# Splitting the first query stacks of two attentions, the first attention's stacks and the seam inside the second mixture

## The chip, the cores and the metric

The kernel runs on one core of a Trainium2 chip. The metric is the device time of one execution in microseconds (us), the median of three runs. The core has five engines that run side by side: TensorE (PE in the profile, with its weight loads as PEld), VectorE (DVE), ScalarE (ACT), GpSimd (POOL) and SyncE (SP, which only issues transfers). They meet through semaphores that the kernel sets and waits for by hand. Instructions of one engine run in the order in which they were written.

## The reference

Four pairs of an attention and a mixture of experts, each added to a residual stream `x` of B x S = 4 x 256 tokens, 128 wide, after a layer norm without weights:

```python
x = x + _L0_xattn_ref(_layernorm(x), ctx_1024, ...)   # 8 heads of 16, lengths mask keys and queries
x = x + _L0_ffn_ref(_layernorm(x), ...)               # shared expert + top 2 of 8, tanh gelu
x = x + _L1_xattn_ref(_layernorm(x), ctx_1024, ...)   # 8 heads of 128, relative positions
x = x + _L1_ffn_ref(_layernorm(x), ...)               # inner norm, mix, norm, then top 2 of 8, silu
x = x + _L2_xattn_ref(_layernorm(x), ctx_1024, ...)   # 16 heads of 8, a 256 x 256 mask
x = x + _L2_ffn_ref(_layernorm(x), ...)               # top 2 of 8, relu
x = x + _L3_xattn_ref(_layernorm(x), ctx_1024, ...)   # 16 heads of 8, biases
x = x + _L3_ffn_ref(_layernorm(x), ...)               # top 1 of 8, gelu
```

An attention is softmax(Q K^T) V and an output projection, with keys and values from `ctx_1024`. An expert is a 128 -> 512 -> 128 network; the mixture adds the results of the best one or two experts of each token, weighted. All is fp32.

## The kernel before, in words

The parts are called `a0, f0, a1, f1, a2, f2, a3, f3` (ORDER, L308): attentions `a`, mixtures `f`. Tokens stand in 8 tiles of 128; a half is 4 tiles (512 tokens), and a sequence (256 tokens) is 2 tiles. Each engine has a function of its own (sync L329, gpsimd L556, vector L708, scalar L1283, tensor L1542), and each walks the parts in ORDER. Within a part all engines run the same loop over steps `i` or `s`, and what is done in which step is written out by hand. A step number therefore fixes what stands before and behind an operation in its engine's queue.

*Narrow attentions* (`a0`, `a2`, `a3`; L816, L1331, L1609). Scores are wanted in fp32 exactness from bf16 matmuls: queries and keys are each split into three bf16 parts (`split`, L784: four VectorE steps), the parts are written to a scratch in HBM (`stack_out`, L354, three DMAs) and read back so that the parts of one head stand below each other in the partitions of `Qs` and `Ks` (`stack_in`, L372). One unit `i` of the loop is one head of one sequence: `scores` on TensorE (L1636), a maximum on VectorE (L878 or L875), GpSimd splits the maxima of four units (`maxima_parts`, L645), TensorE turns them (`turn_maxima`, L1651, from unit 6), ScalarE copies them and, in `a2` and `a3`, SP sends them into rows of `Qs` (L402). Then come the shifted scores (L1669, LAG units later), exponentials (L1363), probabilities times values (L1688), a transpose, normalising, an output transpose, the projection (L1716) and the residual (L856). In `a0` the queries come by halves and the keys at once; in `a2` and `a3` the first half of the queries is made in the mixture before, and the second half within the attention, at unit SECOND_HALF = 13, since the second half of `x` is only then combined (`combine`, L892).

*Mixtures* (`mixture`, L1073, L1423, L1819). Each half goes through: norm (`norm_stats`, `norm_apply`, with the power by GpSimd, `layer_norm_rstd` L592), transpose (`turn_norm`), ScalarE's copy (`copy_T`), `logits` (L1573), `choose` (L915, which experts), `ranks` (L1755), `slots` (L936, each token's row in a list sorted by expert), `plan_blocks`. GpSimd scatters the rows (`send_rows` L614, one indirect DMA for each tile and rank), SP reads the sorted rows (`rows_in`, L459) in quads of four blocks of 128, TensorE turns a quad (L1825) and does one block a step: `up_block(s - 1)` (L1835) and `down_block(s - 2)` (L1864), with ScalarE's activation between them. Blocks 8 and up of a half ("more") take an expert that is chosen at run time: VectorE copies its weights one step ahead (`fetch_weights`, L1081). VectorE adds a quad's biases (`finished`, L1092), SP writes it back (`y_out`, L470), GpSimd gathers the rows of each token (`fetch_results`, L624) and VectorE adds them to `x` (`combine`, L992). There are nb = 19, 15, 15 and 11 blocks a half in `f0` to `f3`, and 2 nb + 2 steps. The first quad of half 1 is turned in step nb - 1 (`quads_at`, L111). In `f1` and `f2` the keys and values of the next attention are made from step 11 on; half 0 is combined and normed for it in step nb + 9 and nb + 10, transposed in nb + 11, made to queries in nb + 12 and split in nb + 13. `f1` has an inner layer before its routing (`inner_layer`, L1241, L1923).

*Queues.* SP's order of transfers is written out (L409 to L552): a wait there holds all transfers behind it. GpSimd's order follows `norms` (L121, L666): behind the norm of `a2.0` stand the gathers of `f1`'s second half, mixed with the first maxima (L674). At the start ScalarE fills `Va` (L1314) and 32 rows of `Qs` (L1317), and VectorE 32 rows of `Ks` (L770).

## Time and profile before

| | us |
|---|---|
| median of three runs | 806.21 |
| lowest, highest run | 806.12, 817.81 |
| profiled execution | 808.12 |
| its span | 806.4 |
| TensorE, VectorE, ScalarE, GpSimd busy | 634.6, 415.5, 373.7, 184.8 |
| chain that ended last: PE, DVE, DMA, POOL, issue, ACT | 48%, 15%, 12%, 9%, 8%, 5% |

Times in the trace count from the start of the span. A row of the timeline has its start, how long its instructions lasted, engine, line and operation, what it writes and reads, how many instructions it merges, and in brackets the engine's idle time before it with what ended it. The chain is followed back from the last instruction, at each step to what released it.

### The profile page before, as it was taken

What the parts mean: (1) busy time and instruction counts of PE and PEld (TensorE: products, weight loads), DVE (VectorE), ACT (ScalarE), POOL (GpSimd) and SP (SyncE); (2) the same over time, 40 slices, a digit from 0 to 9 for tenths busy, and PEclk for the clock granted to TensorE, in tenths of its full rate; (3) what the DMA queues carried; (4) which work ended last, traced back from release to release, by engine and by line L of the source; (5) the groups of instructions that cost most, each with busy time, mean ns of one, the idle gap of its engine ahead of it and who ended that gap; (6) DMA issues with size and microseconds to landing.
All of it is one profiled execution on the core that took longest, in us unless ns stands there. A gap on an engine that the chain in (4) does not pass through costs nothing.

```text
span 806.4 us, 14301 instructions
## 1 busy us (share of the span) xinstructions
PE 634.6 (79%) x4784; PEld 486.8 (60%) x4784; DVE 415.5 (52%) x1410; ACT 373.7 (46%) x930; POOL 184.8 (23%) x352
## 2 busy tenths in 40 slices
PE   4398659998898988687756589987997469978790
PEld 2165459886665666586755347755996324546790
DVE  6675533524266678656123567772544277873320
ACT  7065225554464546764443146653332126755460
POOL 1234313030040010413120411132313051131111
PEclk8599679999999999989797679997998759998996
DMA  5894089110677771201491313324174413431211
GB/s 155 252 358 158 13 166 189 33 37 27 163 244 217 230 213 53 76 14 50 148 144 53 75 43 73 112 90 89 54 202 79 102 31 85 154 102 43 76 50 49
DMA packets 92978, 90.76 MB, mean 113 GB/s; under 512 B 10980, under 2 KB 83301, under 8 KB 92716
## 3 DMA queue, kind: packets, MB, share of 16 engines
q1 hardware_dynamic: 89324, 82.51, 38.0%
q0 software_dynamic: 3584, 7.35, 3.6%
q8 instruction: 40, 0.66, 0.3%
q14 instruction: 30, 0.25, 0.1%
HBM read 53.06 MB, written 35.59 MB: 110 GB/s over the span
## 4 chain that ended last, share of the span: by engine, by line
PE 48%; DVE 15%; DMA 12%; POOL 9%; issue 8%; ACT 5%; SPq 1%; DVEq 0%; POOLq 0%; ACTq 0%
PE bank L1854 10%; PE bank L1875 9%; PE bank L1696 4%; PE bank L1644 3%; DMA late<-rows_sorted,idx 3%; PE bank L1679 3%; POOL rows_sorted L621 3%; PE bank L1983 2%; PE bank L1790 2%; DMA rows_sorted<-stage 2%; DVE negmax L878 2%; PE bank L1950 2%; POOL xm L631 2%; PE bank L1831 1%; POOL late L631 1%
## 5 line engine op out<-in xcount | busy, mean ns | idle before, releaser
L1875 PE MATMUL bank<-W,spare 128*128 128x128 f32 (+1 forms) x960 | 132.9, 284 | 1.4 <-ACT spare L1447 0.9
L1875 PEld LDWEIGHTS bank<-W,spare 128*128 128x128 f32 x960 | 122.8, 200 | 3.2 <-issue 2.1
L878 DVE TENSOR_REDUCE negmax<-bank 128x2 f32<-128x512 f32 x128 | 85.3, 689 | 48.7 <-PE bank L1644 32.0
L1644 PE MATMUL bank<-big 128*128 128x256 bf16 x320 | 73.3, 306 | 36.7 <-DMA big<-parts_scratch 26.0
L1363 ACT ACTIVATE late<-bank 128x512 f32<-128x512 f32 x120 | 70.8, 595 | 56.6 <-PE bank L1684 26.9
L1447 ACT ACTIVATE spare<-bank,W 128x128 f32<-128x128 f32 x224 | 64.0, 372 | 41.5 <-PE bank L1854 41.5
L621 POOL DMA_INDIRECT rows_sorted<-xn,idx x56 | 55.6, 992 | 109.2 <-DVE idx L955 94.6
L1679 PE MATMUL bank<-big 128*128 128x256 bf16 x320 | 74.6, 284 | 2.6 <-ACT late L1363 1.2
L1644 PEld LDWEIGHTS bank<-big 128*128 128x128 bf16 x320 | 28.6, 105 | 65.8 <-issue 36.7
L1495 ACT ACTIVATE big<-big,r 128x256 f32<-128x256 f32 x64 | 31.9, 500 | 45.8 <-DVE r L1189 45.7
L1696 PE MATMUL bank<-late 128*32 128x256 f32 x480 | 44.7, 399 | 0.1
L1560 PE MATMUL bank<-ident,xn 128*128 128x128 f32 x64 | 14.7, 355 | 35.0 <-DVE xn L733 21.8
L1983 PE MATMUL bank<-big,QKT 128*128 128x128 f32 x256 | 34.7, 278 | 8.8 <-DVE x_res L1204 7.4
L631 POOL DMA_INDIRECT late<-rows_sorted,idx x24 | 22.8, 952 | 73.3 <-DMA rows_sorted<-QKT 35.9
L1679 PEld LDWEIGHTS bank<-big 128*128 128x128 bf16 x320 | 29.9, 101 | 16.0 <-ACT late L1363 3.8
L1983 PEld LDWEIGHTS bank<-big,QKT 128*128 128x128 f32 x256 | 31.1, 191 | 11.0 <-issue 9.1
L1350 ACT ACTIVATE nmT<-bank 12x256 bf16<-12x256 f32 x40 | 14.5, 363 | 47.2 <-PE bank L1655 47.1
L653 POOL CAST nmp<-negmax 128x8 bf16<-128x8 f32 x40 | 7.6, 191 | 122.7 <-DVE negmax L878 70.6
L1560 PEld LDWEIGHTS bank<-ident,xn 128*128 128x128 f32 x64 | 9.6, 169 | 41.8 <-issue 26.0
L595 POOL TENSOR_SCALAR rstd<-mv 128x4 f32<-128x4 f32 x20 | 5.2, 258 | 127.7 <-DVE mv L726 127.6
L1854 PE MATMUL bank<-stage,W 128*128 128x128 f32 x256 | 33.8, 275 | 0.0
L1189 DVE CUSTOM_DVE_ANT_0 big<-bank,late 128x256 f32<-128x256 f32 x64 | 24.4, 420 | 18.2 <-PE bank L1953 13.7
(280 smaller groups left out, 1372.6 us busy)
## 6 DMA issues: line engine op xcount, KB each, us to landing
W<-in_f_wx SPq DMA_DIRECT2D x25, 578.0 KB, 7.2
late<-bands_scratch SPq DMA_DIRECT2D x8, 1024.0 KB, 5.5
W<-in_f_wx SPq DMA_DIRECT2D x8, 514.0 KB, 3.5
bands_scratch<-zrow SPq DMA_DIRECT2D x4, 768.0 KB, 12.7
big<-parts_scratch SPq DMA_DIRECT2D x6, 512.0 KB, 5.5
stage<-rows_sorted SPq DMA_DIRECT2D x11, 256.0 KB, 3.3
rows_sorted<-stage SPq DMA_DIRECT2D x11, 256.0 KB, 3.3
parts_scratch<-big SPq DMA_DIRECT2D x3, 768.0 KB
```

The source lines that it names most:

```text
L621: pool.indirect_dma_start(rows_sorted[hf], bass.IndirectOffsetOnAxis(idx[:, k, t:t + 1], 0), xn[:, t, :], None)\
L631: pool.indirect_dma_start(gathered(key, hf)[:, t, k, :], None, rows_sorted[hf], bass.IndirectOffsetOnAxis(idx[:, k, 4 * hf + t:4 * hf + t ...
L878: ins = v.tensor_reduce(negmax[:, g % 2, :, j], bank[i % 2][:, :].rearrange("p (t k) -> p t k", t=2), AX.X, ALU.max, negate=True)
L1363: a.activation(PTs[j % NPT][:, :, :], bank[2 + j % 2][:, :].rearrange("p (c q) -> p c q", c=2), ACT.Exp)\
L1447: ins = a.activation(hidB[n % 3][:, c, :], src[:, 128 * c:128 * (c + 1)], func, bias=b1r[:, c:c + 1])
L1495: a.activation(Pw[2 * (i % 2) + j], negS[2 * (i % 2) + j], ACT.Exp, bias=r1[:, k:k + 1], scale=-1.0, accum_out=r2[:, k:k + 1]).then_inc(se ...
L1644: ins = mm(o, Qs[:, h, S * b + 128 * t:S * b + 128 * (t + 1)], Ks[:, h, S * b:S * (b + 1)], start=True, stop=not mask)
L1679: ins = mm(o, Ks[:, h, S * b + 128 * c:S * b + 128 * (c + 1)], Qs[:, h, S * b:S * (b + 1)], start=True, stop=key == "a3")
L1696: ins = mm(dst[32 * j:32 * (j + 1), 0:256], Va[:, 2 * b + c, h + j, :], PTs[(4 * g + j) % NPT][:, c, :], start=c == 0, stop=c == 1)
L1854: ins = mm(dst[:, 128 * c:128 * (c + 1)], w[:, 128 * c:128 * (c + 1)], rhs, start=True, stop=True)
L1875: ins = mm(dst[:, 128 * place_:128 * (place_ + 1)], hidB[n % 3][:, c, :], w2[:, 128 * c:128 * (c + 1)], start=c == 0, stop=c == FC - 1)
L1983: ins = mm(dst[:, 128 * j:128 * (j + 1)], PTw[i % 2][:, 256 * j + 128 * c:256 * j + 128 * (c + 1)], Vp[:, 2 * b + c, 128 * (2 * p + j):128 ...
```

## The change

It does six things. (1) Start: the stacks of `a0` go by halves, keys too; the fills of the rows of `Qs` and `Ks` are both ScalarE's, as fp32 copies, and `Va` is filled behind the first queries; VectorE's fill is gone. (2) `f0`: in `a0`'s loop `copy_T`, `logits`, `choose`, `ranks` and `slots` of half 0 stand one to three steps earlier, and logits ahead of the step's attention work. In every mixture the logits of half 1 stand at the head of their step. (3) `f1`: the inner layer's end, logits and choice of half 1 two steps earlier (a clear by ScalarE moves from step 6 to 8); the first quad of half 1 is turned in step nb + 1, behind the down block of the step before; on SP `y_out("f1", 0, 3)` stands ahead of `rows_in("f1", 1)`. (4) `a2` and `a3`: the first half's queries are made in two pieces, "0" (sequence 0) and "h" (sequence 1), each with norm, transpose, queries, split and stack of its own; `combine` of half 0 goes by two tiles; gathers and maxima alternate on GpSimd. (5) SECOND_HALF is 15. (6) `f3`: `rows_in("f3", 1)` ahead of `y_out("f3", 0, 1)`. Semaphores are merged and renamed to make room. The core of the diff (left out: renamed semaphores, and helpers that put the pieces' tile and column ranges in place of `4 * hf`):

```diff
 MASK_ROW = 96
 MAX_ROW = 80
-SECOND_HALF = {"a2": 13, "a3": 13}
...
             starts = [(hf, q, max(hf * all_blocks[key] + SHARED[key] + 4 * q - 1, 0)) for hf in range(2) for q in range(quads[key])]
+            starts = [(hf, q, all_blocks[key] + 1 if (key, hf, q) == ("f1", 1, 0) else at_step) for hf, q, at_step in starts]
             return [(hf, q) for hf, q, at_step in starts if at_step == s]
 
...
         COUNTS["x"] = [("a0", B), ("a1", NT), ("a2", B), ("a3", B)]
 
@@ -278,6 +281,34 @@
                 return stage
             return {"f0": big[:, 8192:10240], "f1": late[:, 4096:6144]}.get(key, QKT)
 
+        def tiles_of(name):
+
+
+            key, hf = name.split(".")
...
-            stack_out("a0", 1)
+            stack_out("a0", 1, 0)
             stack_out("a0", 0, 0)
-            stack_in("a0", 1)
+            stack_in("a0", 1, 0)
             stack_in("a0", 0, 0)
+            stack_out("a0", 1, 1)
             sp.wait_ge(sem("c.maskrow"), 1)
             sp.dma_start(Ks[MASK_ROW:MASK_ROW + 1, 1:8, :], Ks[MASK_ROW:MASK_ROW + 1, 0:1, :].broadcast_to([1, 7, TOK]))\
               .then_inc(sem("ld.mask"), 16)
-            stack("a0", 0, 1)
-            sp.wait_ge(sem("c.zrow"), 1)
+            stack_out("a0", 0, 1)
+            stack_in("a0", 1, 1)
+            stack_in("a0", 0, 1)
+            sp.wait_ge(sem("c.zrow"), 2)
...
             rows_in("f1", 0)
             for q in range(3):
                 y_out("f1", 0, q)
+            y_out("f1", 0, 3)
             rows_in("f1", 1)
-            y_out("f1", 0, 3)
             def attention_transfers(key, before, nxt):
 
+                stack(key, 0, 0)
                 y_out(before, 1, 2)
-                stack(key, 0, 0)
+                stack_out(key, 0, "h")
                 y_out(before, 1, 3)
+                stack_in(key, 0, "h")
                 sp.wait_ge(*at(before, "bd", 2 * all_blocks[before]))
...
             attention_transfers("a3", "f2", "f3")
             rows_in("f3", 0)
             y_out("f3", 0, 0)
+            rows_in("f3", 1)
             y_out("f3", 0, 1)
-            rows_in("f3", 1)
             y_out("f3", 0, 2)
...
-                if name in ("a2.0", "a3.0"):
-                    fetch_results(BEFORE[name[:2]], 1, [0, 1])
-                    maxima_parts(name[:2], [0])
-                    fetch_results(BEFORE[name[:2]], 1, [2])
-                    maxima_parts(name[:2], [1])
-                    fetch_results(BEFORE[name[:2]], 1, [3])
-                    maxima_parts(name[:2], [2])
+                if name in ("a2.h", "a3.h"):
+                    for t in range(4):
+                        fetch_results(BEFORE[name[:2]], 1, [t])
+                        if t < 3:
+                            maxima_parts(name[:2], [t])
...
             v.memset(zrow[:, :], 0.0).then_inc(sem("c.zrow"), 1)
-            v.memset(spare[96:128, 0:256].bitcast(bf16), 1.0).then_inc(sem("c.ones"), 1)
-            link(v.memset(big[96:128, 8192:12288], 0.0))
+            v.memset(spare[96:128, 0:256].bitcast(bf16), 1.0).then_inc(sem("c.zrow"), 1)
...
@@ -821,10 +856,11 @@
                     x_ready(dve, key, 0)
                     norm_stats(key, 0, x)
                     norm_apply(key, 0, x, xn)
-                    for c in range(2):
-                        dve.wait_ge(*at(key, "kt", c + 1))
-                        split(KT, slice(512 * c, 512 * (c + 1)), "kp")
+                    dve.wait_ge(*at(key, "kt", 1))
+                    split(KT, slice(0, 512), "kp")
                     query_parts(key, 0)
+                    dve.wait_ge(*at(key, "kt", 2))
+                    split(KT, slice(512, TOK), "kp")
                     x_ready(dve, key, 1)
...
-                    if i == 2 * H + L + 18:
+                    if i == 2 * H + L + (15 if key == "a0" else 18):
                         choose(ffn_key, 0)
-                    if i == 2 * H + L + 21:
+                    if i == 2 * H + L + (18 if key == "a0" else 21):
                         slots(ffn_key, 0)
...
-                    first = 9 if key == "f1" else 3
+                    first = 7 if key == "f1" else 3
...
-                    if s == nb + (9 if key in NEXT else 8):
+                    if key in NEXT:
+                        if s == nb + 7:
+                            combine(key, 0, (0, 1))
+                            norm_stats(nxt, 0, x)
+                        if s == nb + 8:
+                            norm_apply(nxt, 0, x, xn)
+                        if s == nb + 10:
+                            combine(key, 0, (2, 3))
+                            x_ready(dve, nxt, 0)
+                            norm_stats(nxt, "h", x)
+                        if s == nb + 11:
+                            query_parts(nxt, 0)
+                            norm_apply(nxt, "h", x, xn)
+                        if s == nb + 14:
+                            query_parts(nxt, "h")
+                    elif s == nb + 8:
                         combine(key, 0)
                         if nxt:
                             x_ready(dve, nxt, 0)
                             norm_stats(nxt, 0, x)
-                    if s == nb + (10 if key in NEXT else 9) and nxt:
+                    elif s == nb + 9 and nxt:
                         norm_apply(nxt, 0, x, xn)
                     ks = KEYS_STEP.get(key, 99)
                     if ks + 1 <= s < ks + 5:
                         keys_parts(nxt, [s - ks - 1])
                     if s == ks + 5:
                         values(nxt)
-                    if s == nb + 13 and nxt in NARROW:
-                        query_parts(nxt, 0)
...
+            ones = spare[96:128, 0:256]
+            act.wait_ge(sem("c.zrow"), 2)
+            a.activation(big[96:128, 0:4096].rearrange("p (k c) -> p k c", c=2 * D),
+                         ones.unsqueeze(1).broadcast_to([32, 16, 2 * D]), ACT.Copy).then_inc(sem("c.rows"), 1)
+            a.activation(big[96:128, 8192:12288].rearrange("p (k c) -> p k c", c=2 * D),
+                         zrow[96:128, :].unsqueeze(1).broadcast_to([32, 16, 2 * D]), ACT.Copy).then_inc(sem("c.rows"), 1)
...
+                    a.activation(Va[:, :, :, :].rearrange("p t h w -> p (t h w)").rearrange("p (k c) -> p k c", c=2 * D),
+                                 zrow[:, :].unsqueeze(1).broadcast_to([128, 16, 2 * D]), ACT.Copy).then_inc(sem("c.Va"), 1)
...
-                        if s == 6:
+                        if s == 8:
                             act.wait_ge(sem("a1.pv"), UNITS)
                             clear(Vp[:, 6:8, :].rearrange("p t (k c) -> p (t k) c", c=2 * D))
-                        if s == 8:
+                        if s == 6:
                             copy_T("f1n", 1, nT[1])
...
-                    if s == nb + 11 and nxt in NARROW:
-                        copy_T(nxt, 0, nT[0])
-                    if s == nb + 12 and nxt in NARROW:
-                        queries(nxt, 0)
+                    if key in NEXT and s in (nb + 9, nb + 12):
+                        copy_T(nxt, 0 if s == nb + 9 else "h", nT[0])
+                    if key in NEXT and s in (nb + 10, nb + 13):
+                        queries(nxt, 0 if s == nb + 10 else "h")
...
                         pe.wait_ge(sem(f"st.q{b // 2}"), 16 + 32 * LAYER_OF[key])
+                    if h == 0 and b == 1 and key != "a0":
+                        pe.wait_ge(sem("st.qh"), 32 * LAYER_OF[key])
+                    if h == 0 and b == 2 and key == "a0":
+                        pe.wait_ge(sem("st.k1"), 16)
...
+                    if key == "a0" and i == 2 * H + L + 15:
+                        logits(ffn_key, 0)
...
                 for s in range(N + 2):
+                    seam = key == "f1" and s == nb + 1
+                    if seam:
+                        down_block(s - 2)
+                    if s == first:
+                        logits(key, 1)
                     for hf, q in quads_at(key, s):
                         turned(hf, q)
...
-                    if s >= 2:
+                    if s >= 2 and not seam:
                         down_block(s - 2)
                     if key == "f1":
-                        if s in (2, 3, 8):
-                            inner_layer(1, (2, 3, 8).index(s))
+                        if s in (2, 3, 6):
...
-                    first = 9 if key == "f1" else 3
-                    if s == first:
-                        logits(key, 1)
...
-                    if s == nb + 11 and nxt in NARROW:
-                        turn_norm(nxt, 0)
-                    if s == nb + 12 and nxt in NARROW:
-                        queries(nxt, 0)
+                    if key in NEXT and s in (nb + 9, nb + 12):
+                        turn_norm(nxt, 0 if s == nb + 9 else "h")
+                    if key in NEXT and s in (nb + 10, nb + 13):
+                        queries(nxt, 0 if s == nb + 10 else "h")
```

## Rows read from the trace of the kernel before

**Rows 1.** Busy time, clock (PEclk) and transfers by stretch; (x) is a number of instructions.

```profile
0.00:37.00 37.00, 13.31 (x33) 7.21 (x34) 23.07 (x63) 15.60 (x10) 7.90 (x22) 0.72 0.75 209
...
414.00:451.00 37.00, 14.09 (x86) 12.06 (x85) 9.91 (x34) 8.27 (x25) 1.53 (x2) 0.71 0.41 82
```

**Rows 2.** Timeline of the start, all engines, 0 to 37 us.

```profile
2.08 3.62 ACT L1314 ACTIVATE late<-zrow 128x4096 f32<-128x4096 f32 x1
...
5.72 7.03 ACT L1317 ACTIVATE big<-spare 32x8192 bf16<-32x8192 bf16 x1
...
6.19 3.74 PE L1594 MATMUL bank<-cT,aw 128*128 128x512 f32 x4 [6.19 <-DMA cT<-in_ctxT]
...
12.77 1.09 ACT L1328 ACTIVATE QKT<-bank 128x512 f32<-128x512 f32 x2
...
15.05 0.69 DVE L782 TENSOR_TENSOR big<-QKT,big 128x512 bf16<-128x512 f32 x1
...
20.33 3.37 SPq L369 DMA_DIRECT2D parts_scratch<-spare  x3
...
36.92 1.01 PE L1644 MATMUL bank<-big 128*128 128x256 bf16 x4 [4.93 <-DMA big<-parts_scratch]
```

**Rows 3.** Timeline, end of the first attention, TensorE and GpSimd.

```profile
85.64 1.03 PE L1581 MATMUL bank<-rw,nT 128*128 128x8 f32 x8 [0.60 <-DVE x_res L859]
...
89.34 0.21 PE L1762 MATMUL bank<-oneh,aw 128*128 128x32 bf16 x1 [2.40 <-DVE oneh L934]
...
93.22 1.25 POOL L621 DMA_INDIRECT rows_sorted<-xn,idx  x1 [16.07 <-DVE idx L955]
```

**Rows 4.** Timeline, the seam inside the second mixture: TensorE, SyncE, GpSimd.

```profile
387.23 1.12 PE L1831 MATMUL bank<-ident,stage 128*128 128x128 f32 x4 [7.47 <-DMA stage<-rows_sorted]
...
388.14 1.92 PE L1854 MATMUL bank<-late,w1copy 128*128 128x128 f32 x8
...
393.59 1.06 PE L1854 MATMUL bank<-stage,W 128*128 128x128 f32 x8
...
396.40 0.36 SPq L474 DMA_DIRECT2D rows_sorted<-late  x1
...
399.34 0.99 POOL L631 DMA_INDIRECT late<-rows_sorted,idx  x1 [16.01 <-DMA rows_sorted<-late]
```

**Rows 5.** Timeline, seam from second mixture to third attention: VectorE, TensorE, SyncE.

```profile
411.84 0.35 DVE L1005 SCALAR_TENSOR_TENSOR x_res<-late,wts,x_res 128x128 f32<-128x128 f32 x1
...
418.08 0.35 DVE L1005 SCALAR_TENSOR_TENSOR x_res<-late,wts,x_res 128x128 f32<-128x128 f32 x1 [5.88 <-DMA late<-rows_sorted,idx]
...
427.23 1.15 PE L1560 MATMUL bank<-ident,xn 128*128 128x128 f32 x4 [12.62 <-DVE xn L733]
...
450.63 0.37 PE L1644 MATMUL bank<-big 128*128 128x256 bf16 x1 [10.07 <-DMA big<-parts_scratch]
...
442.85 1.31 SPq L382 DMA_DIRECT2D big<-parts_scratch  x2
```

**Rows 6.** Timeline, seam from third mixture to fourth attention: GpSimd, VectorE, TensorE.

```profile
600.94 0.98 POOL L631 DMA_INDIRECT late<-rows_sorted,idx  x1 [18.50 <-DMA rows_sorted<-QKT]
...
614.36 2.32 DVE L1005 SCALAR_TENSOR_TENSOR x_res<-late,wts,x_res 128x128 f32<-128x128 f32 x7 [1.92 <-DMA late<-rows_sorted,idx]
...
620.24 1.16 PE L1560 MATMUL bank<-ident,xn 128*128 128x128 f32 x4 [5.68 <-DVE xn L733]
...
642.88 1.01 PE L1644 MATMUL bank<-big 128*128 128x256 bf16 x4 [11.04 <-DMA big<-parts_scratch]
```

**Rows 7.** Transfers issued from 395 to 452 us: count, KB each, median us to landing.

```profile
big<-parts_scratch SPq DMA_DIRECT2D x1, 1024.0 KB, 13.7
...
rows_sorted<-stage SPq DMA_DIRECT2D x1, 192.0 KB, 6.4
...
late<-rows_sorted,idx POOLq DMA_INDIRECT x8, 14.0
...
xm<-rows_sorted,idx POOLq DMA_INDIRECT x1, 2.6
```

**Rows 8.** Timeline of TensorE, the seam inside the last mixture.

```profile
760.66 1.09 PE L1831 MATMUL bank<-ident,stage 128*128 128x128 f32 x4 [4.26 <-DMA stage<-rows_sorted]
```

157 lines of the change are left out of this document (90 added, 67 removed).

## The prediction

> **What bounds the kernel now.** I first read the table by stage, for TensorE's clock and idle time. TensorE is busy for 634.6 of 806.4 us, but not evenly [rows 1]. In the first 37 us it works 13.3 us, at a mean clock of 0.72; in 414 to 451, the seam from the second mixture to the third attention, 14.1 of 37 us at 0.71. So the time to be had lies where chains of small steps and transfers leave TensorE empty. Then I read what each first matmul after an empty stretch had waited for. Start: ScalarE fills two constant regions before its first key copy (ends 5.7 and 12.75), the copy starts at 12.77 although the keys' matmuls end at 9.93, and the first score is at 36.92, behind a DMA [rows 2]. Routing of the first mixture: logits start at 85.64, after the probabilities, projection and residual of the attention; slots are known at 92.3 and the first row is sent at 93.22 [rows 3]. Second mixture: TensorE waits 7.47 us for the second half's rows at 387.23 [rows 4]. First seam: 12.62 us for `xn` at 427.23 and 10.07 us for the query stack at 450.63 [rows 5]. Second seam: 5.68 and 11.04 us [rows 6]. Last mixture: 4.26 us at 760.66 [rows 8]. The six waits from 387 us on add up to 51.1 us; none is arithmetic. (The third attention is `a2`, the fourth `a3`.)
>
> **The change, part by part.** Times below are on the old trace's scale; each part's gain is carried along.
>
> *Start.* ScalarE does the 32-row fills as 4096 fp32 columns each. One 4096-column fill took 3.62 us, one of 8192 bf16 columns 7.03 [rows 2], so the two now end at 2.08 + 2 x 3.62 = 9.3 in place of 12.75; the third (`Va`) moves behind the first queries. The key copy then starts at 9.3, waits a moment for its matmul, and the first half's parts are split at 12.3 (a split of 512 columns took 2.3 us: it began behind the copy's first half, at 13.4, and its last step ended at 15.74 [rows 2]). The query chain (transpose, copy, matmul 2.07, copy 0.60, split 2.3) gives query parts at 16.7, where they were ready at 20.33 [rows 2]. Before, 4.5 MB went out and in between 18.0 and 36.9, with the DMA engines full. Now 3.0 MB must pass before the first score, and 0.75 MB of second-half keys slips in: 18.5 x 3.75/4.5 = 15.4 us from 12.8, so 28.2, and the mask row, issued at about 26 behind VectorE's second norm, lands near 30. First score: 30.7, a gain of 6.2 (bounds 3 and 8). What is late next is the second half's stack: parts at 33.4, two reads after the writes, landing near 44 to 46 (a read of 0.75 MB took 7.8 us from its first issue in the first seam [rows 5]), needed 14 us after the first score, at 45. I take 1 us off: 5.
>
> *First mixture's routing.* Logits go ahead of the transposes, probabilities and projection; the choice (VectorE, 2.6 us, from the logits' end at 86.67 to the ranks at 89.34 [rows 3]) then runs under them. The copy of the transposes could be done at 80.2, so logits end at 81.2, which delays the attention's work by 1.3 us. Ranks then wait for the residual of that group at about 86.1, not for the choice at 89.3 [rows 3]. Gain: 89.34 - 86.25 = 3.1. The second half's norm follows (it waited for the slots' bank until 92.4), and GpSimd's eight sends and one `rstd` shift with it. I take 3 (bounds 0, if the attention's end decides, and 5).
>
> *Second mixture.* Inner norm, logits and choice come two steps earlier. Two blocks are 3.6 us, but logits wait for their copy, and VectorE's weight copy of that step waits for the hidden block behind them: I get the slots at 370.1 for 372.4, rows sent at 380.1 + 2.3 = 382.4. At the seam three down and two up blocks (5 x 0.9 = 4.5 us) now run before the wait. Against this, on SP the last result write of half 0 goes ahead of `rows_in` of half 1, so rows wait for the last down block (384.9), three additions and 0.4 us of issue: received at 388.8, later than 387.23 [rows 4]. But at that moment only one transpose group stands before block 15, which comes at 390.6 in place of 393.6, though at the lower of the clock's two levels, 1.2 GHz: the same eight matmuls took 1.92 us at 388.14, behind the wait, and 1.06 at 393.59 [rows 4]. Old block 15 ran fast, the new one slow; with that counted, block 16 ends at 393.7 for 396.3. Shift: 2.6 us. The result write starts at 386 and not 396.40, so GpSimd's gathers start at 388.5 and not 399.34.
>
> *First seam.* The key stack's transfers, too, are issued 8.5 us earlier. The gathers took 14.0 us to land there and 2.6 us in the next attention [rows 7]. The first tile was consumed at 411.84, the second at 418.08 [rows 5]. If all moves by 8.5 us, tile 1 lands at 409.6; as its gathers now go out ahead of the key stack's read, it may land up to 6 us sooner. So 403.5 to 409.6, and only tiles 0 and 1 are needed at step 22. Adding, half the norm and `rstd` (3.5 us): transpose at 409.3 to 413, where TensorE is ready at 408.0, and not 427.23. Remaining: 13 blocks' halves at 0.9 = 11.7, small pieces 1.3, lower clock 0 to 2: the mixture ends at 422.5 to 428 (before 440.56). The first sequence's query parts are ready at 416 to 421, since the queries come five steps before the end; out 3.4 us, in 5 (from the first issue at 442.85 it was 7.8 us for twice the columns [rows 5]): 424.5 to 430. First score at 427.5 in the middle, before 450.63: gain 23, the 2.6 included (bounds 15 and 27).
>
> *What is given back in the third attention.* GpSimd now fetches a tile before the first maxima, and first waits for the last result write, which stands behind the first read and the "h" write on SP. It landed just as scores began, now some 3.5 us after. Tile 0 (2.5 us) and its maxima parts (1.1 us) are then done at 7.1, for a turn due at 6.7 us after the first score; the four tiles, each 2.5, with three maxima parts, end near 20 with landing, and `combine` at unit 15 comes at 16 to 17. VectorE waits about 3 us there, and a score needs its maximum. Cost 3 (bounds 0 and 8).
>
> *Second seam.* Gathers are not moved here (600.94, tile 1 consumed at 614.36 [rows 6]). With two tiles the transpose goes at 617.9, 2.3 earlier, but four more block halves (3.6 us) lie behind it: the mixture ends at 633.4, 1.6 later than before. The query stack is ready at 634.5, in place of 642.88: gain 8.4 (bounds 4 and 10). Given back in the fourth attention, where VectorE's reductions, one a unit, set the pace and nothing hides a wait: 3.5 (bounds 0 and 8).
>
> *Logits at the head of their step in mixtures 1, 3, 4.* TensorE waits 0.85 us for the copy, and no longer 0.78 for the choice: nothing. In the last mixture, slots come 1.3 us earlier and `rows_in` no longer stands behind a result write: rows at 757.7 for 760.66, and less idle time before them. Gain 3 (bounds 1 and 4). Renamed semaphores and the two moved clears: nothing, since ScalarE still does each within the wait for the next block; without that cover a clear costs its own length once.
>
> *A rule weighed against the trace.* In the seam the gathers were slow only while SP's queue was full [rows 7]. The Trainium skill (DMA: Bandwidth & Descriptors, "Queues, rings and completion order") says that each DMA engine takes the queues that have work in turn, packet by packet; the trace's 14.0 against 2.6 us agrees. By that rule the order on either queue counts for little and the whole knot moves, so tile 1 would land 8.5 us earlier, at the late end of the interval above, which lengthens the sum's gap before the transpose by 3 us. The same page ("Rules for kernel authors") asks for transfers of 1 MiB or more; the change halves them, and no row before shows a piece of 256 columns. If pieces were no faster than halves, each stack would cost 1.5 us more, 3 in all.
>
> **Sum.** 5 + 3 + 23 - 3 + 8.4 - 3.5 + 3 = 35.9. The profiled execution took 808.12, 1.7 more than its span of 806.4; the sum gives it 772.2. The median of the runs was 806.21, so the forecast is 806.2 - 35.9 = 770 us, rounded.
>
> **The rivals.** (A) *Transfers keep their length.* The knot at the first seam moves whole (first score at 432, 18.5 gained), both given-back terms are 6, and the start waits 3 for the second stack: 3 + 3 + 18.5 - 6 + 7 - 6 + 2 = 21.5, 785 us. For it: the pieces keep their number of rows, and the gathers' 14.0 us shows full queues. Against: the key stack's read landed after 13.7 us and half as many bytes after 7.8 [rows 5, 7]. (B) *The earlier order frees more.* Gathers land before the key stack is read at all, no transpose waits, and TensorE keeps its clock through both short gaps: 7 + 4 + 27 - 1 + 10 - 1 + 4 = 50 less 3 for late second halves, 759 us. Against: after each wait of over 4 us shown the first matmuls ran at 1.2 GHz (1.92 us for eight [rows 4]). (C) *Slower: maxima behind results.* In both attentions `maxima_parts` of group 0 stands on GpSimd behind the last result write, itself behind two stack transfers on SP. If it lands L us after the first score, the stall is L + 3.6 - 6.7. The gains outside are 42.4; it decides from 21.2 a seam, L = 24. The worst landing of a read here, 13.7 us [rows 7], taken twice (read and result) with a write of 3 between, begun 2 us before the first score, gives L = 28: stalls of 25 each, 806.2 - 42.4 + 50 = 814 us. Against: in the old seam the same write landed after 6.4 us, behind a whole read [rows 7]. (D) *The change does less than it says:* the choice is early, but in the seams another wait (weights copied by VectorE while it stands at `combine`) takes all but 12 us: 794.
>
> **Chances.** Forecast 0.53 (own range 764 to 777), A 0.22, B 0.16, C 0.04, D 0.05. The range 757 to 787 takes in A and most of B. Two per cent, about what a measurement can tell from no change, is 16 us: faster 0.91, within 0.06 (D and some of C), slower 0.03.
>
> **What would show it.** First score near 31; `choose` of mixture 1 under the probabilities; in mixture 2 block 15 right behind the wait; the gathers starting 10 us before block 23; TensorE idle under 5 us before the `a2.0` transpose and under 4 before each first score; VectorE waiting for a gather at unit 15 in both attentions. A first score above 435 on the old scale, or stalls over 8 us in an attention, would prove the forecast wrong.

## The result, and the profile after

The changed kernel took 778.42 us (median of four runs, 772.52 to 783.57) beside 806.16 for the kernel before: a ratio of 0.9674, with a 95% interval of 0.9571 to 0.9777. By the medians it is 28 us faster, by the ratio 26. A later session of three rounds gave 777.76 beside 807.42 us, a ratio of 0.9652 (0.9614 to 0.9689): 30 and 28 us. The forecast was 770 with a range of 757 to 787: right in sign and inside the range, with 36 us forecast and 26 to 30 measured. Ratios, here and below, leave out the executions marked slow (one of `rows_first`, 789.91 us, and one of the kernel before, 2087 us, in each of the last two sessions), while medians keep them.

The first profiled execution took 783.57 us (span 781.8), the one of the later session 774.13 (span 772.4). Both are used below, since they differ by 9 us for the same program. Line numbers are those of the changed kernel, and in the experiments those of each run's own kernel.

The start, timeline (ScalarE, VectorE, TensorE), answers to [rows 2]:

```profile
5.60 3.60 ACT L1369 ACTIVATE big<-zrow 32x4096 f32<-32x4096 f32 x1
9.22 1.09 ACT L1380 ACTIVATE QKT<-bank 128x512 f32<-128x512 f32 x2
...
29.26 1.06 PE L1706 MATMUL bank<-big 128*128 128x256 bf16 x4
34.00 3.27 PE L1706 MATMUL bank<-big 128*128 128x256 bf16 x10 [3.68 <-DVE negmax L914]
...
31.78 0.69 DVE L817 TENSOR_TENSOR spare<-QKT,spare 128x512 bf16<-128x512 f32 x1
...
33.27 0.67 DVE L914 TENSOR_REDUCE negmax<-bank 128x2 f32<-128x512 f32 x1
```

The first score is at 29.26, 7.7 us earlier. But two units on, TensorE stands for 3.68 us: VectorE is still at the second half's query parts and the masks, and its first maximum starts at 33.27. What is carried on is 3.7 us: the first matmul with the values is at 43.89, before at 47.57.

Routing of the first mixture, timeline, TensorE and GpSimd, answers to [rows 3]. Logits no longer wait for the residual, the ranks (82.70) do:

```profile
82.70 0.18 PE L1826 MATMUL bank<-oneh,aw 128*128 128x32 bf16 x1 [0.61 <-DVE x_res L895]
...
102.87 1.11 PE L1896 MATMUL bank<-ident,big 128*128 128x128 f32 x4 [5.42 <-DMA big<-rows_sorted]
...
86.41 1.25 POOL L657 DMA_INDIRECT rows_sorted<-xn,idx  x1 [12.95 <-DVE idx L991]
```

The seam inside the second mixture and the first seam, timeline, TensorE, SyncE, GpSimd and VectorE, answers to [rows 4, 5]:

```profile
383.45 1.15 PE L1940 MATMUL bank<-W,spare 128*128 x8 [0.44 <-ACT spare L1502]
388.99 0.99 PE L1896 MATMUL bank<-ident,stage 128*128 128x128 f32 x4 [4.38 <-DMA stage<-rows_sorted]
...
410.43 0.49 PE L1614 MATMUL bank<-ident,xn 128*128 128x128 f32 x2 [0.91 <-DVE xn L768]
...
426.13 0.27 PE L1706 MATMUL bank<-big 128*128 128x256 bf16 x1
...
433.40 0.29 PE L1717 MATMUL bank<-identb,nmp 128*12 128x128 bf16 x2 [2.22 <-POOL nmp L692]
...
447.52 0.39 PE L1706 MATMUL bank<-big 128*128 128x256 bf16 x1 [2.81 <-DVE negmax L914]
...
385.46 0.36 SPq L508 DMA_DIRECT2D rows_sorted<-late  x1
385.86 2.17 SPq L500 DMA_DIRECT2D stage<-rows_sorted  x4
...
388.32 0.99 POOL L667 DMA_INDIRECT late<-rows_sorted,idx  x1 [8.25 <-DMA rows_sorted<-late]
...
363.01 0.43 DVE L1128 COPY big<-W 128x516 f32 x1 [6.17 <-ACT spare L1502]
...
384.75 0.69 DVE L1149 TENSOR_TENSOR late<-bank,W 128x128 f32<-128x128 f32 x3 [1.84 <-PE bank L1940]
...
406.36 0.43 DVE L1128 COPY big<-W 128x516 f32 x1 [3.70 <-ACT spare L1502]
406.71 1.26 DVE L1041 SCALAR_TENSOR_TENSOR x_res<-late,wts,x_res 128x128 f32<-128x128 f32 x4
```

TensorE no longer waits for a query stack at all before the third attention (10.07 before), and 0.91 us for the norm where it was 12.62. The row reads (L500) stand behind the last result write (L508), which waits for VectorE's additions of 384.75. The additions of tiles 0 and 1 (L1041, 406.71) wait for no gather: the last gather of tile 1 had landed at 400.85.

Second seam and fourth attention, timeline, TensorE and SyncE, answers to [rows 6]:

```profile
598.60 0.66 PE L1614 MATMUL bank<-ident,xn 128*128 128x128 f32 x2 [5.91 <-DVE xn L768]
...
615.85 0.60 PE L1706 MATMUL bank<-big 128*128 128x256 bf16 x4 [0.26 <-DMA big<-parts_scratch]
...
622.45 0.38 PE L1717 MATMUL bank<-identb,nmp 128*12 128x128 bf16 x2 [2.65 <-POOL nmp L692]
...
636.85 0.39 PE L1706 MATMUL bank<-big 128*128 128x256 bf16 x2 [3.21 <-DVE negmax L914]
```

The DMA issues of 365 to 440 us, in the columns of [rows 7]. The query stack of one sequence is read by two issues, of 256 and 128 KB, and there are two such stacks. The first began at 420.77 and was in at 425.55, 4.8 us later; in [rows 5] the read of a half, twice the bytes, began at 442.85 and was in at 450.39, 7.5 us later:

```profile
big<-parts_scratch SPq DMA_DIRECT2D x1, 1024.0 KB, 13.1
...
big<-parts_scratch SPq DMA_DIRECT2D x2, 256.0 KB, 4.1
...
big<-parts_scratch SPq DMA_DIRECT2D x2, 128.0 KB, 4.4
...
late<-rows_sorted,idx POOLq DMA_INDIRECT x8, 7.7
```

In the last mixture TensorE waits 2.55 us for the second half's rows (4.26 in [rows 8]).

Now the sum. Each stage is the time between two instructions that both kernels have; the gain is its length in the profile of before less its length here, and below zero where the stage got longer:

| Stage (from the instruction before, to) | Forecast | First profile | Later profile |
|---|---|---|---|
| first matmul with values | 5 | 3.7 | 3.4 |
| first rows of mixture 1 turned | 3 | 2.7 | 2.7 |
| first rows of mixture 2 turned | 0 | -1.0 | -0.4 |
| its second half's rows turned | -1.6 | -7.2 | -6.5 |
| first score of attention 3 | 24.6 | 26.3 | 26.6 |
| first rows of mixture 3 (give-back) | -3 | -3.0 | -2.2 |
| first score of attention 4 | 8.4 | 5.5 | 11.7 |
| first rows of mixture 4 (give-back) | -3.5 | -6.2 | -6.7 |
| second half's rows of mixture 4 | 3 | 3.8 | 3.9 |
| last block | 0 | 0.0 | 1.6 |
| sum | 35.9 | 24.7 | 34.0 |

(The 23 us forecast for mixture 2 and the seam are rows four and five together.) Five of the nine us between the two profiles lie in the third mixture, ahead of any wait that the change touches. The windows of its first 48 us say why. The first profile:

```profile
532.00:580.00 48.00, 45.41 (x331) 43.15 (x332) 19.99 (x68) 15.22 (x26) 9.07 (x10) 0.82 0.39 109
```

and the later one:

```profile
531.00:579.00 48.00, 46.20 (x383) 44.19 (x383) 19.79 (x65) 17.39 (x29) 11.23 (x13) 0.94 0.47 125
```

TensorE is as busy in both, but at a mean granted clock of 0.82 it gets through 331 instructions and at 0.94 through 383. One profile is therefore not enough to size a term of a few us. The kernel before has one profile alone, so that its own scatter is in every row of the table.

### The profile page after: what moved, and what is told of

Read it like the earlier page. It is cut to its first block, busy times and chain, and to the rows that moved or that the text cites. A ratio compares the mean times of both kernels' runs of the same rounds, so it can differ in the third digit from the quotient of the medians.

```text
span 781.8 us, 14348 instructions
## 1 busy us (share of the span) xinstructions
PE 640.2 (82%) x4788; PEld 493.5 (63%) x4788; DVE 412.6 (53%) x1417; ACT 374.5 (48%) x935; POOL 185.7 (24%) x356
## 4 chain that ended last, share of the span: by engine, by line
PE 53%; DVE 14%; POOL 9%; DMA 8%; issue 8%; ACT 5%; SPq 0%; POOLq 0%; DVEq 0%; ACTq 0%
PE bank L1919 12%; PE bank L1940 10%; PE bank L1758 3%; PE bank L1706 3%; PE bank L1741 3%; PE bank L2050 2%; POOL rows_sorted L657 2%; PE bank L2017 2%; PE bank L1854 2%; PE bank L1896 2%; POOL xm L667 2%; PE bank L1879 2%; DVE negmax L914 2%; PE bank L1614 1%; POOL rstd L632 1%
## 5 line engine op out<-in xcount | busy, mean ns | idle before, releaser
L631 POOL TENSOR_SCALAR rstd<-mv 128x4 f32<-128x4 f32 (+1 forms) x22 | 5.6, 254 | 132.4 <-DVE mv L761 132.4
L1919 PE MATMUL bank<-stage,W 128*128 128x128 f32 x256 | 35.5, 285 | 0.7 <-ACT stage L1488 0.7
L1614 PE MATMUL bank<-ident,xn 128*128 128x128 f32 x64 | 14.4, 338 | 26.0 <-DVE xn L768 11.7
L1919 PEld LDWEIGHTS bank<-stage,W 128*128 128x128 f32 x256 | 33.1, 201 | 3.5 <-issue 2.4
L2017 PE MATMUL bank<-big,nT 128*128 128x512 f32 x64 | 34.5, 623 | 0.0
```

What stands on the lines that cost most here:

```text
L1919: ins = mm(dst[:, 128 * c:128 * (c + 1)], w[:, 128 * c:128 * (c + 1)], rhs, start=True, stop=True)
L2017: mm(dst[:, :].rearrange("p (h k) -> p h k", h=2), nT[0][:, 128 * t:128 * (t + 1)], U[:, 2 * p:2 * p + 2, S * b:S * (b + 1)], start=True, ...
```

## The experiments

Twelve kernels ran, four to a session, each with three rounds beside the kernel before. Stage times are from their profiles; "the yardstick" is the changed kernel run again, in the first of the three sessions. The second session ran on another chip (the kernel before took 810.34 us there, 807.42 in the first), and its stages are set beside the yardstick's.

**The yardstick.**

> The changed kernel once more, as the yardstick for the others on the same chip. In the two profiles taken so far it is 24.6 us faster by its span; by my sum of stages the gains are 3.7 us at the start, 2.7 in the first routing, -1.0 up to the second mixture, -4.2 inside the second mixture up to its last group of rows, 23.3 from there to the third attention's first score, -3.0 in the third attention, 5.5 to the fourth attention's first score, -6.2 in the fourth attention and 3.8 in the last mixture. If these are properties of the kernel, each comes back within 1 us. Rival: the losses inside the second mixture (-4.2) and in the fourth attention (-6.2) are scatter of one execution; then one of them comes back at least 2 us smaller.

Measured: 777.76 us, ratio 0.9652 (0.9614 to 0.9689). Both disputed losses came back (-6.5 and -6.7, by the stages of the table above; the expectation cuts the second mixture at a later row); what did not was the 5 us in the third mixture, and that was the clock.

**Row reads first.**

```
-            y_out("f1", 0, 3)
             rows_in("f1", 1)
+            y_out("f1", 0, 3)
```

> In the second mixture SP issues the second half's row reads ahead of the last result write of the first half. Theory 1 (my reading of the trace): the reads were late because they stood behind that write, which waits for the additions that end at 385.44; the sends had ended at 380.1, so the reads are issued at about 381.5 and land near 384.7, when TensorE's last block before them ends. The wait of 4.38 us at the turn of those rows goes, and the kernel is 3.5 to 4.4 us faster. The gathers stay where they are, at 388.3. Theory 2: the reads are bound by the row sends' own landing, not by the order on SP; then the wait stays over 3 us and the time is the same.

Measured: 779.83 us, 0.9652 (0.9613 to 0.9692): no different from the yardstick. TensorE's timeline:

```profile
383.92 0.66 PE L1896 MATMUL bank<-ident,stage 128*128 128x128 f32 x4 [0.84 <-DMA stage<-rows_sorted]
...
408.65 0.66 PE L1614 MATMUL bank<-ident,xn 128*128 128x128 f32 x2 [6.46 <-DVE xn L768]
```

Theory 1 was right on the wait (4.36 us in the yardstick, 0.84 here) and wrong on the end: the transposes stay where they were (yardstick 408.55), and the wait before them grows from 0.92 to 6.46. The gathers start at 387.91, but landed a median of 13.1 us after issue, against 6.7 in the same window of the yardstick. The key stack's read (1 MB and 512 KB) had moved forward too, from 395.44 to 391.48, into the gathers: the last gather of tile 1, issued at 391.71, landed at 405.16, while the three ahead of it took 5.4 to 8.7 us.

**And the key read behind the gathers.**

```
-            y_out("f1", 0, 3)
             rows_in("f1", 1)
+            y_out("f1", 0, 3)
             stack_out("a2", 1)
+            y_out("f1", 1, 0)
             own_in()
             stack_in("a2", 1)
-            y_out("f1", 1, 0)
```

> Like rows_first (row reads ahead of the last result write), and in addition the reads of the third attention's key stack and own rows go behind the second half's first result write, so that they start after GpSimd has issued the eight gathers. Theory 1: in rows_first the wait of 4.4 us at the rows went, but the first transposes of the next attention stayed at 408.65, since the gathers then took 13.1 us beside the key read (6.7 us in the changed kernel): the gathers and the 1 MB read share the transfers. Without the read beside them the gathers take about 2.6 us each, tile 1 is there by 398, the wait of 6.5 us before the transposes goes, and the third attention's first score comes 5 to 6 us earlier than in rows_first (about 420 for 425.5); the stack, read at about 396 to 410, is in time. Theory 2: the gathers are slow for a reason of their own (their list, the landing of the result write); then they keep 7 to 13 us and nothing is gained.

Measured: 777.65 us, 0.96 (0.9532 to 0.9669). TensorE's timeline, and the gathers' line of the DMA issues of 370 to 430 us:

```profile
384.23 0.66 PE L1896 MATMUL bank<-ident,stage 128*128 128x128 f32 x4 [1.06 <-DMA stage<-rows_sorted]
...
404.45 0.49 PE L1614 MATMUL bank<-ident,xn 128*128 128x128 f32 x2 [0.92 <-DVE xn L768]
...
423.07 0.28 PE L1706 MATMUL bank<-big 128*128 128x256 bf16 x1 [2.81 <-DMA big<-parts_scratch]
```

```profile
late<-rows_sorted,idx POOLq DMA_INDIRECT x8, 2.8
```

Theory 1 holds for the gathers: nearly the same start (388.48), 2.8 us to landing and not 13.1, because one read starts later (at 398.96). The norm is there 4.2 us earlier than in rows_first. Only 2.5 of them reach the first score (423.07 for 425.54), where 5 to 6 were expected: the query stack takes over as the last wait. Its write landed 3.8 us after issue (2.2 in the yardstick), beside the delayed key read, which was in at 416.42. Against the changed kernel the whole is 4 us faster by ratio, and the two intervals overlap. The Trainium skill (DMA: Bandwidth & Descriptors, "Queues, rings and completion order") has each DMA engine serve its queues in turn, packet by packet; 13.1 against 2.8 us agrees.

**The seam inside the second mixture undone.**

```
-            starts = [(hf, q, all_blocks[key] + 1 if (key, hf, q) == ("f1", 1, 0) else at_step) for hf, q, at_step in starts]
...
-                    seam = key == "f1" and s == nb + 1
+                    seam = False
...
-            y_out("f1", 0, 3)
             rows_in("f1", 1)
+            y_out("f1", 0, 3)
```

> The changed kernel without its edit inside the second mixture: the second half's first rows are turned at their old step, and its row reads stand on SP ahead of the last result write of the first half, which then waits for a down block behind those rows, so that the gathers start near 399 less 5.5, that is at about 393 to 395 (388.3 with the edit). Theory 1 (the prediction's): this edit carries the first seam, by the gathers' start; without it tile 1 lands 6 to 8 us later, the transposes of the third attention wait for it, and its first score comes 4 to 7 us later, at 430 to 433. Theory 2: the edit gives with one hand what it takes with the other (it costs 6.5 to 7 us at the rows): then the rows are turned 3 to 5 us earlier, and the first score comes within 2 us of 425.

Measured: 790.69 us, 0.9752 (0.9687 to 0.9817). Timeline, TensorE and GpSimd:

```profile
416.56 0.66 PE L1613 MATMUL bank<-ident,xn 128*128 128x128 f32 x2 [9.87 <-DVE xn L767]
...
395.35 0.99 POOL L666 DMA_INDIRECT late<-rows_sorted,idx  x1 [16.54 <-DMA rows_sorted<-late]
```

Theory 1, with more than its price: the rows are turned at 383.26, 4.7 us before the yardstick's, and still the first score comes at 434.47, 9.7 later (by ratio the whole kernel is 8 us slower). Eight us of gathers' start (387.31 in the yardstick), and a landing of 13.1 in place of 6.7, are worth more than the wait at the rows costs. The late landing is again that of the gathers beside the key read: tile 1's last gather was issued at 399.15, the read at 399.23, and it landed at 413.08.

**The second half two units earlier.**

```
-SECOND_HALF = {"a2": 15, "a3": 15}
+SECOND_HALF = {"a2": 13, "a3": 13}
```

> SECOND_HALF is 13 again in both attentions: weights, additions, norm and queries of the second half two units earlier. Theory 1 (the prediction's account of what is given back): VectorE then waits 1.5 to 3 us more for the last tile's gather at the additions, because results land about 3 us after the first score and not at it; SP gets the query parts two units earlier, so group 4's rows are not held up. The one takes about what the other gives, and both attentions stay within 1.5 us. Theory 2: the two units more are what costs (the stack write on SP): then the fourth attention is 2 to 4 us shorter.

Measured: 774.5 us, 0.9587 (0.9523 to 0.9651). TensorE's timeline of the fourth attention (first score 608.20), then the yardstick's (607.60):

```profile
629.05 0.59 PE L1706 MATMUL bank<-big 128*128 128x256 bf16 x2 [6.12 <-DVE negmax L914]
...
650.03 0.39 PE L1741 MATMUL bank<-big 128*128 128x256 bf16 x2 [1.88 <-DMA big<-nmT]
```

```profile
628.47 0.57 PE L1706 MATMUL bank<-big 128*128 128x256 bf16 x2 [3.57 <-DVE negmax L914]
...
651.33 0.39 PE L1741 MATMUL bank<-big 128*128 128x256 bf16 x2 [3.13 <-DMA big<-nmT]
```

Half of each theory. VectorE does wait longer for the last gather, as Theory 1 said. But the attention is 3.4 us shorter (93.9 for 97.4), as Theory 2 said, and the longer wait costs nothing: in both kernels it ends 20.9 us after the first score, when the gather has landed, so that two units more ahead of the additions only put the query parts later. The time between the exponentials of units 16 and 24 is 9.05 us here, 11.75 in the yardstick and 8.28 before. That is where the rows of maxima groups 4 to 6 go out on SP beside the second half's stack. (From unit 0 to unit 16 both kernels take some 3 us longer than the one before, 25.6 and 26.2 for 23.1; that part is the late gathers'.) SP's queue, yardstick:

```profile
641.78 0.81 SPq L437 DMA_DIRECT2D big<-nmT  x1
643.86 1.29 SPq L413 DMA_DIRECT2D big<-parts_scratch  x2
645.20 11.91 SPq L437 DMA_DIRECT2D big<-nmT  x3
```

The read is issued 36.3 us after the first score in the yardstick, 34.0 in half_at_13 and 31.6 before. So the moved constant, which the prediction treated as part of the gathers' account, is a loss of its own in the fourth attention. In the third it showed only 0.6 us. By ratio the kernel is 5 us faster than the changed one, but the intervals overlap; the 3.4 us rest on the profiles.

**The stack around group 5.**

```
-                    if g == 4:
+                    if g == 5:
                         stack_out(key, 0, 1)
                     maxima_to_rows(key, g)
-                    if g == 4:
+                    if g == 5:
                         stack_in(key, 0, 1)
```

> In the third and fourth attention SP issues the second half's query stack around the rows of maxima group 5 and not of group 4. Theory 1: of the 6.2 to 6.7 us that the fourth attention is longer, some 3 are SP's order: its stack write waits for query parts that now come at unit 20 and not 18, and the rows of group 4 (ready at 29.5 us after the first score, issued at 34.2) stand behind it; the next group's rows then stand behind the read and land late (TensorE waits 3.13 us for them, 1.10 before the change). With the stack one group later, group 4 is issued at about 30.5 and the fourth attention is 2 to 3 us shorter, the third 0 to 1. Theory 2: the rows land late because the 384 KB read is beside them wherever it stands; then the wait moves to group 6 and keeps its 3 us, and nothing changes.

Measured: 783.77 us, 0.9695 (0.9633 to 0.9757). Both attentions are longer (gains -3.8 and -7.4 for -2.2 and -6.7 in the yardstick); the whole kernel is slower by ratio, but the intervals overlap. Group 4's rows go out 1.3 us earlier after the first score (32.9 for 34.2), and then the stack itself is missed at unit 32, in TensorE's timeline:

```profile
655.65 0.61 PE L1706 MATMUL bank<-big 128*128 128x256 bf16 x2 [4.38 <-DMA big<-parts_scratch]
```

Neither theory named this. Rows and stack both have to pass between the query parts and unit 32; half_at_13, which has the parts earlier, helped, and this other order did not.

**Maxima ahead of the fetches.**

```
-                        fetch_results(BEFORE[name[:2]], 1, [t])
                         if t < 3:
                             maxima_parts(name[:2], [t])
+                        fetch_results(BEFORE[name[:2]], 1, [t])
```

> On GpSimd, in the third and fourth attention, the maxima parts of groups 0, 1 and 2 go ahead of the fetches of tiles 0, 1 and 2. Theory 1: the waits of 2.22 and 2.65 us at the first turn of the maxima come from the fetch of tile 0 ahead of them and go; tile fetches then follow 2 us later, so the waits at the additions of unit 15 (2.81 and 3.21 us) grow by about 2: the sum is between 1 us faster and 1 us slower. Theory 2: the turn waits for the maxima themselves; then its wait stays and the additions wait longer: 3 to 4 us slower.

Measured: 780.86 us, 0.9679 (0.9647 to 0.9711). TensorE's timeline in the fourth attention:

```profile
614.96 0.28 PE L1717 MATMUL bank<-identb,nmp 128*12 128x128 bf16 x2 [0.16 <-POOL nmp L692]
...
632.12 0.61 PE L1706 MATMUL bank<-big 128*128 128x256 bf16 x2 [6.23 <-DVE negmax L914]
```

Theory 1: the first wait goes (2.65 to 0.16), the one at the second turn grows from 0.50 to 1.55 and the one at the additions from 3.57 to 6.23, and each attention is about 1 us longer. The order on GpSimd trades one wait for the other.

**First maxima ahead of the second half's queries.**

```
                     values(key)
-                    query_parts(key, 1)
-                    masks()
...
                         ins.then_inc(sem("nm"), 1)
+                    if key == "a0" and i == 3:
+                        query_parts(key, 1)
+                    if key == "a0" and i == 7:
+                        masks()
```

> In the first attention VectorE splits the second half's queries after the maxima of unit 3, and makes the masks after those of unit 7, in place of both before unit 0. Theory 1: what delays the first maximum (33.27, with the first score at 29.26) is VectorE's own order. Then the first maximum starts near 30.3, the first values' matmul (43.89) comes 2.5 to 3 us earlier, and the second half's query stack, 2.8 us later than now, still lands before unit 16 needs it: 2 to 3 us faster in all. Theory 2: the second half's stack is what the first attention waits for next; then TensorE waits at unit 16 by about what was gained, and the time is the same or slower.

Measured: 779.91 us, 0.9668 (0.9623 to 0.9712). TensorE's timeline:

```profile
30.23 1.01 PE L1708 MATMUL bank<-big 128*128 128x256 bf16 x4 [0.55 <-DMA big<-big]
...
36.38 0.61 PE L1708 MATMUL bank<-big 128*128 128x256 bf16 x2 [2.58 <-DVE negmax L912]
```

Neither theory. The first maximum starts at 30.86, 2.4 us earlier than in the first profile, and the first matmul with values stays at 43.87. VectorE's 2.3 us of splitting and 0.9 of masks come onto the path wherever they stood among the first maxima (here 2.58 us at 36.38); in the kernel before they ran while TensorE waited for the query stack.

The last four ran on a chip on which every kernel was slower (the one before took 839.33 us), so they are compared among themselves.

**Routing undone** (choice, ranks, copy and logits of the first mixture at their old steps).

```
-                    if i == 2 * H + L + (15 if key == "a0" else 18):
+                    if i == 2 * H + L + 18:
                         choose(ffn_key, 0)
...
-                    if key == "a0" and i == 2 * H + L + 15:
-                        logits(ffn_key, 0)
```

> The changed kernel with the first mixture routed at its old steps (logits behind the transposes and probabilities, choice three units later). Theory 1: routing is worth what the profile shows between the first values' matmul and the first mixture's rows, 2.7 us; those rows come at 105.5 to 106.3 for 103.2, and the kernel is 2 to 3 us slower. Theory 2: the sends decide; the rows come within 0.5 us of 103.2.

Measured: 815.84 us, 0.9722 (0.9653 to 0.9792). The first rows are turned at 106.00, in the other three kernels of the session at 102.90 to 103.03: 3.0 us. Theory 1. The session has no run of the changed kernel, so that the whole times say nothing on 3 us.

**Queries' first half in one piece.** SECOND_HALF goes back to 13 with it.

```
-SECOND_HALF = {"a2": 15, "a3": 15}
+SECOND_HALF = {"a2": 13, "a3": 13}
...
-            if key in ("a2", "a3"):
-                return {"0": range(0, 2), "h": range(2, 4), "1": range(4, 8)}[hf]
...
-                stack(key, 0, 0)
                 y_out(before, 1, 2)
-                stack_out(key, 0, "h")
+                stack(key, 0, 0)
                 y_out(before, 1, 3)
-                stack_in(key, 0, "h")
...
-                        if s == nb + 7:
-                            combine(key, 0, (0, 1))
+                        if s == nb + 9:
+                            combine(key, 0)
```

> The changed kernel with the queries' first half as one piece again (additions, norm, transposes, queries, parts and stack of four tiles at the old steps, the old order of fetches and maxima on GpSimd, SECOND_HALF 13); everything else, the seam inside the second mixture too, as changed. Theory 1: the pieces carry what the first seam gains behind the gathers and nearly all of the second seam. Then TensorE again waits 8 to 11 us for the query stack before both first scores; the third attention's first score comes 6 to 9 us later than 424.8 and the stretch from the third mixture's first rows to the fourth attention's first score is 8 to 11 us longer than 76.9; the attentions give back 2 to 3 us less each: 8 to 14 us slower than the changed kernel, near 786 to 791. Theory 2: the earlier gathers alone are most of it and the pieces only move the wait: within 5 us of the changed kernel.

Measured: 822.23 us, 0.9817 (0.9769 to 0.9865), by ratio 13 us slower than the yardstick. TensorE's timeline:

```profile
454.21 0.37 PE L1696 MATMUL bank<-big 128*128 128x256 bf16 x1 [9.60 <-DMA big<-parts_scratch]
...
652.42 1.01 PE L1696 MATMUL bank<-big 128*128 128x256 bf16 x4 [10.17 <-DMA big<-parts_scratch]
```

Theory 1: both waits for the query stack are back. Beside route_undone, which has the pieces, the stretch from mixture 2's first rows to attention 3's first score is 8.5 us longer and the one from mixture 3's to attention 4's 6.8. The attentions are 5.4 and 6.6 us shorter, but three things are mixed in that. route_undone has SECOND_HALF at 15. In its attentions VectorE and ScalarE also stood idle 3.9 and 3.8 us for no engine of the core, where whole_half did not (ScalarE, timeline, near the end of the fourth):

```profile
735.69 0.60 ACT L1418 ACTIVATE late<-bank 128x512 f32<-128x512 f32 x1 [3.83 <-remote]
```

The third is what the pieces themselves give back. With SECOND_HALF at 13 in both, the wait at the additions of the fourth attention ends 17.8 us after the first score in whole_half, as in the kernel before, and 20.8 in the kernel labelled both, pieces and all: 3 us for the late results. Over the whole attention only 0.5 of it is left (94.4 and 94.9), with a wait of TensorE near the end, 2.0 us in either, that the profile puts to no engine.

**The two gains together, and the second seam too.** The first is keys_late and half_at_13 in one; the second adds:

```
-            stack_out("a3", 1)
             y_out("f2", 0, 3)
+            stack_out("a3", 1)
+            y_out("f2", 1, 0)
             stack_in("a3", 1)
-            y_out("f2", 1, 0)
```

> keys_late and half_at_13 together: row reads first and the key stack's read behind the second half's first result write in the second mixture, and SECOND_HALF 13. Theory 1: the two gains lie in different stretches and add up. By the profiles, keys_late has its third attention's first score at 423.07, 1.7 us earlier than the changed kernel's yardstick, and half_at_13 has a fourth attention 3.4 us shorter: a span near 767 to 769, about 4 to 5 us below the changed kernel. Rival: what half_at_13 gains depends on when the last results land, and keys_late moves the results of the second mixture nearer to the first score; then the third attention gives back 2 us and the sum is only half_at_13's.

> As the kernel labelled both, and in the third mixture the last result write of the first half goes ahead of the fourth attention's key stack write, and the key stack's read behind the second half's first result write. Theory 1: the second seam has the same contention as the first: its gathers start at 583.0 in the changed kernel's first profile, TensorE waits 5.9 us for their sums before the fourth attention's transposes. With the result write ahead of 768 KB of stack and the 1 MB read behind the gathers, they land 5 to 8 us earlier and the wait goes: 4 to 6 us faster than the kernel labelled both, if the key stack, read from about 580, is in by the first score. Theory 2: the wait before the first score takes it over, as in keys_late (2.81 us there): 1 to 3 us. Theory 3: nothing, since the gathers' start is bound by the last down block of the first half.

Measured: 800.45 us, 0.9577 (0.9505 to 0.965), and 798.82, 0.9553 (0.9486 to 0.9621). The fourth attention is 94.9 and 95.1 us long where route_undone's is 101.0, with the 3.8 us of idle time in it. The second seam's edit moved the gathers' start by 1 us (597.85 for 598.80) and the stretch to the first score by 0.4. VectorE's timeline, first both, then both_f2_keys:

```profile
611.03 1.00 DVE L1041 SCALAR_TENSOR_TENSOR x_res<-late,wts,x_res 128x128 f32<-128x128 f32 x3 [2.12 <-DMA late<-rows_sorted,idx]
```

```profile
610.46 0.43 DVE L1128 COPY big<-W 128x516 f32 x1 [8.00 <-ACT spare L1498]
```

The start is bound as Theory 3 said, since the write waits for its down block. But the landing is not: in both VectorE waits 1.49 and 2.12 us for gathers, in both_f2_keys not at all, and TensorE's wait before the transposes goes from 1.51 us to nothing. What stands in its place is a stall of ScalarE of 3.7 us, in both kernels, for no engine of the core, and at the first score a wait of 1.46 us for the stack (0.38 in both). What this edit is worth without that stall is open. Against 0.9652 for the changed kernel, 0.9553 would be 8 us; but the intervals touch and the session differs, so that these kernels beat the changed one is likely and not shown.

The edits at the start and in the last mixture were not undone; their gains are read off the stages.

## Why the prediction was right, and where it was off

**The main mechanism.** "Chains of small steps and transfers leave TensorE empty" and the seams carry the gain: shown. Undoing the seam inside the second mixture cost 9.7 us at the next first score, undoing the pieces 8.5 and 6.8. Rival B is out (no profile sums to 50 us). Rival C did not happen: the first turn of the maxima waits 2.2 to 2.7 us, not 25. Rival D, 12 us in all, is out at 26 to 30. Rival A's premise, that transfers keep their length, is false at 4.8 us for the read of a piece where that of a half took 7.5; its total, 785, misses by 7.

**The start (5, measured 3.4 to 3.7).** The first score came earlier than forecast (29.26 for 30.7). The step that failed is "what is late next is the second half's stack": late next was VectorE's queue, 3.2 us of parts and masks that the old wait had covered. TensorE did not wait for the second stack.

**Routing (3, measured 2.7; 3.0 by undoing it).** Right, step by step: ranks wait for the residual.

**Second mixture and first seam (23, measured 19.1 and 20.1).** Two steps were off. "I get the slots at 370.1" failed: on the old scale (5.4 us added) they came at 374.4, because `choose`, brought forward, stands on VectorE behind a weight copy that waited 6.17 us for a hidden block. That did not set the rows' time, though: in rows_first they are turned at 383.92 with the same sends. "Received at 388.8" became 394.4 because the reads stand behind the last result write, and the last down block ahead of it, put at 384.9, ended at 390.0. TensorE needed 49.6 us from the first rows to the end of that block, where the kernel before needed 39.3 to its last block ahead of the wait and the five added ones were counted as 4.5. Waits of over 0.4 us in that stretch are 6.8 us in sum and were 4.6, and the mean granted clock is 0.87 where it was 0.91; the two windows, TensorE alone, after and before:

```profile
335.00:384.60 49.60, 42.76 (x307) 0.87 0.12 37
```

```profile
340.40:379.80 39.40, 34.65 (x267) 0.91 0.11 34
```

The seam behind it gave about 2 more than forecast: the transpose at 410.43 is 415.9 on that scale (forecast 409.3 to 413), but no wait is left before the first score. The gathers' landing did not go as the prediction had drawn it from the rule on queues, by which "the whole knot moves". The gathers start 5.6 us earlier on the old scale (393.8 for 399.34, forecast 388.5), and yet tile 1 is in at 406.3 for 418.05, in the middle of the forecast interval, since its last gather now goes out ahead of the key stack's read and takes 8.7 us for 14.9. So the order of issue counted for much, where the prediction had inferred that it counts for little; rows_first and keys_late say the same. The 14.0 us of [rows 7] are a median of eight: tile 0's two gathers had taken only 5.0 and 6.2.

**Third attention (3, measured 3.0 and 2.2).** The size is right, in part by luck. The wait at unit 15 is 2.81 us, as forecast, but the kernel before already had 2.49 at its unit 13. What is new is 2.22 us at the first turn, which the prediction had put at 0.4 (7.1 for 6.7).

**Second seam (8.4, measured 5.5 and 11.7).** The waits were called rightly (11.04 to 0.26 us). In the nine profiles outside the last session, all with the pieces, the gain goes from 5.5 to 11.7 us with a median of 9.2, so that the forecast fits and one execution's clock hid it.

**Fourth attention (3.5, measured 6.2 to 6.7).** The term that was mis-sized most. The price of late gathers was about right, 3 us (the exponentials of units 0 to 16 take 26.2 us for 23.1); another 3.4 is the second half's stack, started two units later: the prediction did not price the later constant on SP's queue.

**Last mixture (3, measured 3.8 and 3.9).** Right.

Of the 8 us between forecast and measurement, the start (about 1.5), the second mixture with its seam (1 to 4) and the fourth attention (3) fell short in every profile that has these stages as changed. The last mixture (1) and in most profiles the second seam gave more than forecast. The rest is within the scatter.

## What to carry to other kernels

When a wait is removed, ask what the other engines did under it: that work comes onto the path, and moving it by a few steps does not take it off again. A transfer moved forward may land in another's way; here a key stack's read of 1.5 MB moved behind eight small gathers brought them in after 2.8 us and not 13.1. And a constant that says "after unit n" is a time only while nothing stands: with the additions bound by a gather, two units later bought nothing and made the stack late.

## What was not expected of the hardware

The same program showed a mean granted clock of 0.82 and of 0.94 over the same 48 us of a mixture, at the same busy time, and 5 us went with it. Why is open. And in the third session the kernel before took 839.33 us for 806 to 810 in the others; there ScalarE and VectorE stood idle 15 to 20 times for over 0.7 us (up to 12.7) for work of no engine of the core, mostly at the same places in all four profiles, and never in the ten profiles of the other sessions. Here ScalarE in the kernel labelled both:

```profile
410.89 2.17 ACT L1502 ACTIVATE spare<-bank,W 128x128 f32<-128x128 f32 x8 [5.26 <-remote]
```

Ratios within that session fit the others; its absolute times do not. A stage in which one kernel has such a stall and the other has not can't be compared there. The cause is open.
